# Attention kernel with its setup as a block of its own, and with the setup woven into the first batches

## The reference

```
mod = (silu(c) @ wmod)                      # c is 16 x 256, wmod 256 x 1536
sa, ca, ga, sb, cb, gb = the six 256-wide parts of mod, one row per batch
ga, gb = sign(g) * max(|g|, 0.25)           # the gates
h = layernorm(x) * (1 + ca) + sa
x = x + ga * attention(h)                   # 8 heads of 64, keys and values from a 64-wide latent
h = layernorm(x) * (1 + cb) + sb
x = x + gb * moe_ffn(h)                     # router, 8 experts, layernorm with gamma and beta
```

## Time and profile before

| | before |
|---|---|
| median of 3 runs | 1432.89 us (1429.55 to 1435.97) |
| the profiled execution's own time | 1432.32 us |
| its span, first to last instruction | 1430.5 us |
| busy PE, DVE, POOL, ACT | 1174.1, 993.4, 974.9, 756.3 us |
| mean granted TensorE clock | 0.892 |

### The profile page before, as it was taken

One profiled execution on the slowest core, in us unless ns is written; L12 is line 12 of the kernel. 1 busy time (PEld: TensorE's weight loads), 2 busy tenths in 40 slices (PEclk: granted clock), 3 DMA queues, 4 the chain that ended last, 5 costly groups with the idle time before them and its releaser, 6 DMA issues. The chain is left out here.

```text
span 1430.5 us, 23916 instructions
## 1 busy us (share of the span) xinstructions
PE 1174.1 (82%) x5985; PEld 789.2 (55%) x5986; DVE 993.4 (69%) x2210; ACT 756.3 (53%) x1485; POOL 974.9 (68%) x1094
## 2 busy tenths in 40 slices
PE   5489999999999999999999999999941173989500
PEld 3255666656666665666656666566531163979500
DVE  2467877777777776777767777676457883677497
ACT  1356675665765656666666656656413232344144
POOL 1247688787878879788797887969752065555258
PEclk7689999999999999999999999999965555989855
DMA  4000010110101101010110101001031103232285
GB/s 131 16 16 25 7 60 13 48 46 16 60 0 59 45 15 51 9 60 22 37 45 15 59 1 46 31 16 45 18 131 23 37 22 86 49 82 51 50 269 173
DMA packets 68157, 70.89 MB, mean 50 GB/s; under 512 B 12848, under 2 KB 63968, under 8 KB 67952
## 3 DMA queue, kind: packets, MB, share of 16 engines
q1 hardware_dynamic: 46480, 47.18, 10.4%
q10 hardware_dynamic: 16896, 16.78, 3.5%
q0 software_dynamic: 4704, 6.11, 2.8%
HBM read 40.35 MB, written 29.45 MB: 49 GB/s over the span
## 5 line engine op out<-in xcount | busy, mean ns | idle before, releaser
L617 ACT ACTIVATE PF<-PS 128x512 f32<-128x512 f32 x512 | 297.9, 595 | 258.8 <-PE PS L845 246.8
L802 DVE TENSOR_REDUCE NMAX<-PS 128x1 f32<-128x512 f32 x512 | 342.7, 682 | 96.5 <-PE PS L854 92.8
L561 POOL TENSOR_TENSOR SF<-SF,PF 128x512 f32<-128x512 f32 x252 | 321.8, 1299 | 16.3 <-ACT PF L617 16.1
L926 PE MATMUL PS<-PF,V 128*64 128x512 f32 x1024 | 248.2, 605 | 0.0
L844 PE MATMUL PS<-Q,K 128*128 128x512 f32 x512 | 223.2, 436 | 3.7 <-ACT PF L617 3.6
L854 PE MATMUL PS<-K,Q 128*128 128x512 f32 x512 | 205.9, 403 | 12.5 <-DVE NMAX L802 10.8
L845 PE MATMUL PS<-Q,K 128*128 128x512 f32 x512 | 202.1, 395 | 0.0
L558 POOL TENSOR_TENSOR SF<-PF 128x512 f32<-128x512 f32 x126 | 162.0, 1302 | 23.5 <-ACT PF L617 23.5
L636 ACT ACTIVATE Q<-PS 64x512 fp32r<-64x512 f32 x256 | 151.6, 592 | 48.5 <-PE PS L93 43.5
L585 POOL TENSOR_TENSOR XL<-XF,XH 128x512 fp32r<-128x512 f32 x63 | 82.7, 1312 | 129.0 <-ACT XH L691 129.0
L844 PEld LDWEIGHTS PS<-Q,K 128*128 128x128 f32 x512 | 96.9, 189 | 120.7 <-ACT PF L617 55.6
(11 more groups left out here) (323 smaller groups left out, 2538.1 us busy)
## 6 DMA issues: line engine op xcount, KB each, us to landing
X<-in_L_attn_x SPq DMA_DIRECT2D x16, 512.0 KB, 3.5
MODB<-mod_rows SPq DMA_DIRECT2D x16, 512.0 KB, 3.7
h_rows<-H ACTq DMA_DIRECT2D x16, 512.0 KB, 3.0
acc_rows<-H ACTq DMA_DIRECT2D x16, 512.0 KB, 4.1
A<-acc_rows SPq DMA_DIRECT2D x16, 512.0 KB, 8.8
out_x<-X SPq DMA_DIRECT2D x16, 512.0 KB, 2.9
W1F<-in_L_ffn_W SPq DMA_DIRECT2D x3, 1024.0 KB, 4.9
W2F<-in_L_ffn_W SPq DMA_DIRECT2D x3, 1024.0 KB, 6.3
```

The lines of the kernel that those rows point to most:

```text
L561: s_sum.done(pool.tensor_tensor(total, total, tile, ALU.add))
L617: s_exp.done(act.activation(PF[:, u % 8, :], st_bank(u), ACT.Exp))
L802: s_mred.done(dve.tensor_reduce(NMAX[:, p % 2, r:r + 1], mx_bank(u), AX.X, ALU.max, negate=True))
L926: last = pe.matmul(num_bank(p)[odd * R:(odd + 1) * R, :], V1[:, vp, c, :], PF[:, k % 8, :], start=(c == 0), stop=(c == TC - 1))
```

## The change

The function `setup` and its block are gone. Its instructions stand in `attention`, partly ahead of the loops over bodies and partly at chosen slots of the bodies -1, 0 and 1. The setup's tiles lie inside `X1`, in the rows of batches 4 and later (`late(...)`), which are loaded later.

- **Loads, by SP:** C, tokens of batch 0, the first 512 columns of `wmod`, WD, WQ, WK, WO, WV, the other 1024 columns of `wmod`, tokens of batch 1, gamma and beta, WR, BR. Each group has a semaphore of its own. The four stores of zero rows follow. The store of `MR` stands at slot 22 of body 0.
- **PE ahead of the bodies:** transposes of silu(c), the transposed modulation (now the only use of the first 512 columns), WD, and A. In body -1: at slot 11 the transposes of WO and the products G; at slot 16 half of the modulation rows, at slot 21 the other half. G is made for two heads at a time: the transposes give 128 rows (two heads), and the products of the even and the odd head use partitions 0 to 63 and 64 to 127 (8 transposes in place of 16; two banks of output in place of four).
- **ACT ahead:** silu, `DH`, and one exponential of a single column. In body -1: `AH` at slot 8, `WOT` (2 copies) at 12, `GH` (2 copies) at 13, four copies of modulation rows out of PSUM at 26.
- **DVE ahead:** padding of `K2` (it was POOL's) and ST. In body -1: `SA`, `CA1`, `DL` at slot 0, `AL` at 9, `GL` at 14; the statistics of batch 1 all stand at slot 13. In body 0: the gates and other rows of `MR` at slots 5 to 15, `SAME` at 20.
- **POOL ahead:** identity and constants. The fill of `Q2`'s padding (64 x 4096) stands at slot 13 of body -1, after batch 0's `NLO`.

```diff
 m["s_xin"] = [PairStream(sem(f"xin{j}"), j) for j in range(2)]
-            setup(nc, ap, m, sem)
             attention(nc, ap, m, sem, sba)
...
+    WQ, WK, WD = late(0, H, D, rows=R), late(2048, H, R, rows=R), late(2560, D, rows=R)
...
+            sp.dma_start(C, ap["L0_c"]).then_inc(s_c, 16)
+            m["s_xin"][0].done(sp.dma_start(X1[:, 0:TC, :], x_rows[:, 0:TC, :]))
+            sp.dma_start(WM[:, :, 0:2 * D], wmod[:, :, 0:2 * D]).then_inc(s_wmt, 16)
+            sp.dma_start(WD, ap["L0_attn_Wkv_down"]).then_inc(s_wa, 16)
...
+            sp.dma_start(WM[:, :, 2 * D:6 * D], wmod[:, :, 2 * D:6 * D]).then_inc(s_wm, 16)
+            m["s_xin"][1].done(sp.dma_start(X1[:, TC:2 * TC, :], x_rows[:, TC:2 * TC, :]))
...
 def body(b, par):        # GpSimd
+                    if isinstance(b, int) and (b, n) == (-1, 13):
+                        s_nlo.wait(pool, 0, KC - 1)
+                        pool.memset(Q2[R:P, :, :].bitcast(F32), 0.0).then_inc(s_pad, 1)
+                        pool.wait_ge(s_pad, 1)
...
 @block.scalar
+            act.wait_ge(s_c, 16)
+            act.activation(SG, C, ACT.Silu).then_inc(s_aset, 1)
+            act.wait_ge(s_pset, WDT)
+            for j in range(2):
+                act.activation(DH[:, :, j * R:(j + 1) * R], wdt_ps, ACT.Copy).then_inc(s_aset, 1)
+            act.activation(C[:, 0:1], C[:, 1:2], ACT.Exp)
             def body(b, par):
+                    if at == (-1, 8):
+                        act.wait_ge(s_pset, A_DONE)
+                        for k in range(KC):
+                            act.activation(AH[:, k, :], PS[:, 4 + k, :], ACT.Copy, scale=float(R) ** -0.5).then_inc(s_aset, 1)
+                        act.wait_ge(s_dset, SA_DONE)
+                    if at == (-1, 12):
+                        act.wait_ge(s_pset, WOT_T)
+                        for j in range(2):
+                            act.activation(WOT[:, 2 * j:2 * j + 2, :], PS[:, 3 * j, :].rearrange("p (j n) -> p j n", j=2),
+                                           ACT.Copy).then_inc(s_aset, 1)
...
 body of VectorE
+                    if at == (-1, 9):
+                        low_queries()
+                    if at == (-1, 14):
+                        low_outputs()
+                    if at == (0, 5):
+                        dve.wait_ge(s_aset, RAW_DONE)
+                        gate_sign(0)
...
-                    for c, nb in due([x - 2 * UNITS for x in STAT_AT], b, n):
+                    for c, nb in due([x - 2 * UNITS for x in STAT_AT], b, n) if at is None or b != -1 else [(c, 1) for c in range(TC) if n == 13]:
...
+            def value_outputs():
+                pe.wait_ge(s_aset, WOT_DONE)
+                for j in range(H // 2):
+                    for odd in range(2):
+                        rows = slice(odd * R, (odd + 1) * R)
+                        last = pe.matmul(pair_ps(j)[rows, :], WV[rows, j, :], WOT[rows, j, :], start=True, stop=True)
+                last.then_inc(s_pset, 1)
             def body(b, par):    # TensorE
+                    if at == (-1, 11):
+                        output_rows()
+                        value_outputs()
+                    if at == (-1, 14):
+                        pe.wait_ge(s_aset, AH_DONE)
+                        pe.wait_ge(s_dset, AL_DONE)
+                    if at == (-1, 16):
+                        pe.wait_ge(s_wm, 16)
+                        modulation(0)
+                    if at == (-1, 21):
+                        pe.wait_ge(s_dset, GL_DONE)
+                        modulation(1).then_inc(s_pset, 1)
+                    if at == (-1, 31):
+                        pe.wait_ge(s_const, 5)
+                        pe.wait_ge(s_keypad, 2)
+                        pe.wait_ge(s_pad, 1)
+                        pe.wait_ge(s_aset, RAW_DONE)
```

More of the change, by code:

```diff
@@ L13 @@
+import math
 from contextlib import ExitStack
@@ L819, in project @@
                 return last
+            pe.wait_ge(s_id, 2)
+            pe.wait_ge(s_aset, SILU)
+            for k in range(KC):
+                last = pe.transpose(silu_ps[:, k, :], SG[:, k * P:(k + 1) * P], IDENT[0:NB, 0:NB])
+            last.then_inc(s_pset, 1)
+            pe.wait_ge(s_wmt, 16)
+            pe.wait_ge(s_dset, ST_DONE)
+            for j in range(4):
+                for k in range(KC):
+                    last = pe.matmul(modt_ps[:, j, :], WM[:, k, j * P:(j + 1) * P], ST[:, k, :], start=(k == 0), stop=(k == KC - 1))
@@ new lines, in _, with modulation @@
+            last.then_inc(s_pset, 1)
+            pe.wait_ge(s_wa, 48)
+            for k in range(KC):
+                last = pe.transpose(wdt_ps[:, k, :], WD[:, k * P:(k + 1) * P], IDENT[0:R, 0:R])
+            last.then_inc(s_pset, 1)
+            for k in range(KC):
+                for h in range(H):
+                    last = pe.matmul(PS[:, 4 + k, h * R:(h + 1) * R], WQ[:, h, k * P:(k + 1) * P], WK[:, h, :], start=True, stop=True)
+            last.then_inc(s_pset, 1)
+            def modulation(j):
+                for k in range(KC):
+                    last = pe.matmul(PS[0:NB, 1 - j, :], ST[:, k, :], WM[:, k, 2 * (j + 1) * D:2 * (j + 2) * D],
+                                     start=(k == 0), stop=(k == KC - 1))
+                return last
@@ new lines, in output_rows @@
+            def output_rows():
+                pe.wait_ge(s_wo, 32)
+                pe.wait_ge(s_dset, SA_DONE)
+                for j in range(H // 2):
+                    for k in range(KC):
+                        last = pe.transpose(pair_ps(j)[:, k * P:(k + 1) * P], WO[:, k, j * P:(j + 1) * P], IDENT[:, :])
+                last.then_inc(s_pset, 1)
+            def value_outputs():
+                pe.wait_ge(s_aset, WOT_DONE)
+                for j in range(H // 2):
+                    for odd in range(2):
+                        rows = slice(odd * R, (odd + 1) * R)
+                        last = pe.matmul(pair_ps(j)[rows, :], WV[rows, j, :], WOT[rows, j, :], start=True, stop=True)
+                last.then_inc(s_pset, 1)
```

285 lines of the change are left out of this document (126 added, 159 removed).

## The result

The changed kernel takes 1400.46 us (median of 4 runs, 1398.31 to 1400.98) against 1432.96 for the kernel before: a ratio of 0.9771 (95% interval 0.9747 to 0.9795). The forecast was 1399.5. Its profiled execution has a span of 1398.3 us, 32.2 less than before.

What follows compares the result with a forecast made beforehand. PE was taken to bound attention from 90 us, behind a serial start-up. Sum: 32.2 - 1.0 + 1.3 + 1.0 - 0.7 = 32.8 us sooner, so 1432.3 - 32.8 = 1399.5 us; range 1394 to 1409.

Steps and rivals of the forecast that it cites:

- What bounds the kernel: Whole kernel: from 90 us attention runs at PE's pace; earlier is start-up, two chains of 42.8 and 14.5 us end to end.
- Loads: Start of the kernel: tokens land at about 5 us, first `wmod` at 6.3, WK at 10.1.
- PE up to A: PE ahead of the bodies: transposed modulation 6.3 to 10.2 us, WD's transposes to 10.5, A from 10.5 to 16.6.
- Tokens hidden behind the weights: Batch 0's statistics and scales: XN ends at 14.4 us, before A; 2 us later would change nothing.
- Behind A: A's end to first latent product: PE's branch with paired G (3.5 us) ends at 25.1, 32.2 us sooner.
- A drain: At G on PE: changing tiling from 128 rows to 64 and back drains the engine; no size given.
- Latent to exponential: First latent product to first exponential, 23.94 us before: modulation rows 1.0 later, removed table load 1.3 sooner.
- The rows' term: Modulation rows on PE, body -1: 3.4 us less about 2.4 of idle time, 1.0 later (bounds 0 and 4.4).
- rival 2: Start-up: the clock releases sooner and doesn't fall before the first exponentials; gain 36 to 38 us, about 1396; chance 0.13.
- Clock: Around the first exponential: less PE idle time may save the clock's fall; 1.0 us sooner, bounds 0 and 3.0.
- Body 0: DVE's added gate, row and SAME instructions, 5.5 us of work: 0.7 us later, bounds 0 and 5.5.
- Nothing else: After body 1 nothing else changes; PE's moved work lands before PE is the bound.

Runs made afterwards that it cites:

- the repeat: The changed kernel run again with no edit, beside the other runs on the same chip: 1399.1 us, ratio 0.976 to the kernel before.
- the edit of the kernel before: The kernel before with only WO's transposes and G made for two heads at a time: 1426.5 us, ratio 0.9952.

## Why the prediction was right

- **What bounds the kernel** held: PE's busy time in the later stretch is unchanged to 0.01 us of 150, and each delay or gain at the first exponential came out at the first load of modulation rows (3.8 and 3.9 us later with the tokens held back, 3.4 and 3.4 sooner with A in pairs).
- **Loads** held within 0.2 us: tokens at 5.1 (5), first part of `wmod` at 6.5 (6.3), WD and WK at 10.2 (10.1).
- **PE up to A** was mis-sized: A took 7.03 us, not 6.1. The old 6.08 contained a first stretch at the full clock, which I had noticed and left out of the number.
- **Tokens hidden behind the weights** held, with 2.8 us of slack: shown by holding them back and by the old order of loads.
- **Behind A** held: G takes 3.65 us in pairs and the latent follows it at 25.89, against 25.1 forecast, the whole miss being A's. A drain, which the prediction left without a price, can't have cost more than about 0.5 us: the latent's first weight load starts 0.73 us after G's last one ends, where the loads within G are 0.19 apart. Whether it cost that is not shown. The latent product came 31.4 us sooner, of 32.2 forecast.
- **Latent to exponential** came out 2.1 us shorter than before, where the sum has 0.3 (1.0 longer for the rows, 1.3 shorter for the table). The rows' term was wrong in sign: they cost nothing and keep the clock from falling at 32. The latent and first query took 3.1 us in place of 4.6, as G had the clock up when they began: rival 2, for that part. The table load is gone from the path (at 11.20 it lies beside A); that PF follows the last copy of Q at once (47.69 to 47.71) and not 1.30 behind it as before (79.91 to 81.21) shows 1.3 us, not the 2.66 of the Trainium skill, "ScalarE: Activation LUTs", What ACT_TABLE_LOAD costs.
- **Clock** behind the first exponential: the bound of 3.0 was nearer than my 1.0. First exponential to first product with the values took 3.8 us in place of 6.3, 2.5 sooner, at 2.4 GHz throughout. With products that only hold the clock in place of the fall near 39.5, the first exponential came 1.6 sooner still; that fall I had not put into the sum.
- **Body 0** held: 0.7. It was right by luck in two respects: there are eleven instructions for gates and rows and not twelve, and with the two for SAME they took 9.3 us and not 5.5 (see below), of which DVE's free time took most. The sign that I had named, PE busy over 98% in body 0, did not come: it was 94.
- **Nothing else** failed: at the first load of modulation rows the gain was 35.3, 2.5 more than the sum, and 1.7 were lost in one batch and 1.4 after attention. The first of these stands at one place in twelve of the thirteen traces of kernels with an edited start, 61.8 to 62.5 us for a batch that took 60.6 before. The thirteenth, without the gates in body 0, took 60.8. In the changed kernel ACT and DVE there both wait for nothing that the profile shows, in the first body behind the loop (from the waits between 860 and 873):
```profile
DVE GATE L638 <- issue: 1.9, 1, 1.9
ACT H L621 <- issue: 1.6, 1, 1.6
```
The trace without the gates still has ACT's wait (1.7 us) and not DVE's, and the other twelve have DVE's (1.8 to 2.0 us). So the lost time goes with DVE's wait, at the start of its statistics, and not with ACT's. That instructions behind the loop lie otherwise in memory and come late is my guess for it; it was not tried, and the cause stays open. The 1.4 after attention came again in the repeat (span behind the last load 392.8 us in both, 391.4 before); the edited kernels with the same numbers have 391.6 to 392.5, and the edit of the kernel before 388.7, so kernels whose work there is the same differ by more than that. Its cause was not looked for.

So the total was closer (32.5 measured, 32.8 forecast) than its terms, and that closeness is luck: the way to the exponential and the clock behind it were too small by 1.8 and 1.5 us, the way to the latent too large by 0.8, and what was left over met losses of 1.7 and 1.4 that I had excluded. The mechanism, two chains laid side by side with G in pairs in front of the latent, is what the traces show.

## What to carry to other kernels

Where a setup block and the first tile's own preparation are each a serial chain, write both chains with times and find where they join; the slack is the difference there (2.8 us here, and a delay of 8.2 came through as 5.45). Not all of the gain is the weaving: G in pairs gave 5.3 us in the kernel before by itself, and the old order of loads cost 4.9 of the gain. Look at what the moved work does to the clock: work put into TensorE's idle time cost nothing and paid (the modulation rows), and work put into another such place (G at slot 26) stood in front of what another engine waited for. Products that use half the rows or columns of the array went in pairs for half the time here, with neighbours in the order on different halves. Here the halves of A also wrote a PSUM bank each; A with one bank for both was not tried.

## What the runs showed of the hardware

- Up to its first recorded turn the profile's clock column reads 1.00 whatever the durations say: with unpaired G the 512-column products from 28.12 to 31.5 are 0.43 us apart, as they are at 42 to 46 in the changed kernel, where the column says 0.50; in the changed kernel they are 0.23 apart at 28 us. The column says 1.00 in both. It was of use only from the first turn that it recorded.
- The same stretch of the same program ran at either level in two executions (G 3.65 and 1.95 us), a spread of 1.6 us at the first exponential and of 1.0 in the span.
- VectorE's small operations on SBUF tiles took up to five times as long while GpSimd added: `MR` by `sign` 0.93 us on average, where the same step took 0.41 from PSUM and SBUF before. The group by line of the changed kernel, 46 to 100 us, and three rows of its timeline:
```profile
L727 DVE TENSOR_TENSOR X<-X 16x256 f32<-16x256 f32 x2 | 1.9, 930 | 0.0
```
```profile
52.29 5.13 POOL L469 TENSOR_TENSOR SF<-SF,PF 128x512 f32<-128x512 f32 x4
52.32 1.39 DVE L721 TENSOR_SCALAR X<-X 16x256 f32<-16x256 f32 x1
...
59.38 0.27 DVE L721 TENSOR_SCALAR X<-X 16x256 f32<-16x256 f32 x1
```
  The two steps of L727 (0.75 us from 56.94, 1.11 from 63.84) end 0.27 and 0.28 us after an instruction of GpSimd on two SBUF tiles ends (57.42 and 64.67): the extra time looks like waiting, not like slower work.
  The Trainium skill, "SBUF — State Buffer", SBUF: two separate sides, says that GpSimd and a VectorE operation with two SBUF inputs (the TENSOR_TENSOR above) or in a two-port mode exclude each other on their shared ports; single cases of the TENSOR_SCALAR here are 1.39 us beside an addition of GpSimd and 0.27 without one, which agrees.
